# Attention over four images: image 0's first attention in two halves of the queries, and the score maxima of images 2 and 3 computed earlier

## The chip, the cores and the metric

One core of one Trainium2 chip runs the whole program. The metric is device time in microseconds (us) of one execution.

## The reference, cut to what matters

Four images of 64 channels and 1024 pixels each go through three steps.

```python
xf = x.reshape(b, c, n)                         # b=4, c=64, n=1024
q, k, v = (einsum('mc,bcn->bmn', w, xf) for w in (wq, wk, wv))   # m=32
att = softmax(einsum('bmi,bmj->bij', k, q), axis=2)              # 1024 x 1024 an image
x = x + einsum('cm,bmn->bcn', wo, einsum('bij,bmj->bmi', att, v))
t = tokens(x)                                   # 4 x 1024 x 64
z = layernorm(t)
t = t + softmax(z z^T) z                        # second attention
z = layernorm(t)                                # router, top 2 of 8 experts
t = t + gated sum of the two chosen experts of z
```

The first softmax has large scores and so needs the maximum of each row; the second one uses a constant shift.

## The kernel before, in words

**Tiles.** An image has 8 tiles of 128 tokens. Attention 1 of an image has two passes. The maxima pass: TensorE makes the scores of a tile with tokens on the partitions (`max_scores`, L465), VectorE reduces each tile to its row maxima (`row_max`, L1070), negates them and splits them in a high and a low part (`negate_max`, L1076 and L1078), TensorE turns them into a row (`max_row`, L474), and ScalarE and VectorE copy one half each of this row into `kst` (L874, L1083). The score pass: the transposed scores with the maximum already subtracted (`scores1`, L483), the exponential on ScalarE (`exp1`, L877) and the weighted sum of the values on TensorE (`weigh_pair1`, two tiles a call, L490). A score tile needs the whole row, so that no `scores1` of an image begins before the last of its maxima. After it come the output projection (`project_out`, L527), the tokens and their layer norm on VectorE (`tokens1`, `stats_of_1`, `normalize1`, with one power on GpSimd), their transposition (`u_transposed`, L538), attention 2 (`scores2` L551 and L552, `exp2` L880, `weigh_pair2` L490), its transposition (`copy_att2` L889 on ScalarE, `att2_transposed` L566 on TensorE), the second norm, the router (`w_transposed`, `route`), the choice of two experts (`top2` on VectorE with `gap_exp`, L905, on ScalarE), and the experts (`experts` L596, `weigh_experts` L1209 on VectorE, sums on GpSimd).

**Before the maxima** of an image its q and k are projected (`project_qk`), rounded by ScalarE (`round_q` L857, `round_k` L860) and split by VectorE (`split_q` L1062, `split_k` L1067); `project_v` (L454, L455) makes the values, which ScalarE copies (`values`, L865 and L869). `round_x` (L854) and GpSimd prepare x.

**The ring.** TensorE writes nearly all results into three buffers of PSUM of two banks each. `ORDER` (L44 to L72) lists every use of the ring in the order of TensorE's program; use n takes buffer n mod 3, and `take` makes TensorE wait until use n - 3 has been read (`release` names the semaphore). So a tile in the list is bound to the one that stands three places ahead of it, whoever reads that one.

**Order.** There is no loop or planner: each engine has its instructions written out in one order, and executes them in it. The order interleaves images. The stages are those of the list: HEAD (load, image 0's maxima), FIRST (image 0's scores 1, image 1's maxima), SECOND (image 1's scores 1), THIRD (image 0's scores 2, image 2's maxima), FOURTH (image 2's scores 1), FIFTH (image 1's scores 2, image 3's maxima, image 0's experts), SIXTH (image 3's scores 1), SEVENTH and EIGHTH (scores 2 of images 2 and 3), TAIL. `keep_clock(n)` (L632) issues n matmuls on a constant tile whose result nobody reads.

Of the kernel before, what the change touches and what calls it, by code (L numbers as in the profile page):

```python
# [24 lines left out]
P = 128  # L25
# [10 lines left out]
DEEP = 4  # L36


def per_tile(name, b):
# [4 lines left out]
HEAD = [("w3", 0), ("q", 0), ("k", 0), ("vx", 0)] + per_tile("mx", 0) + [("q", 1), ("k", 1), ("mr", 0)]  # L44

FIRST = [("st0", 0), ("st1", 0), ("mx0", 1), ("st2", 0), ("mx1", 1), ("st3", 0), ("mx2", 1), ("mx3", 1), ("st4", 0),
         ("mx4", 1), ("st5", 0), ("mx5", 1), ("st6", 0), ("mx6", 1), ("st7", 0), ("mx7", 1), ("vx", 1), ("mr", 1),
         ("po", 0)]
# [4 lines left out]
THIRD = [("s0", 0), ("s1", 0), ("po", 1), ("mx0", 2), ("s2", 0), ("mx1", 2), ("s3", 0), ("mx2", 2), ("s4", 0),  # L53
         ("mx3", 2), ("s5", 0), ("q", 3), ("uT", 1), ("mx4", 2), ("s6", 0), ("k", 3), ("mx5", 2), ("s7", 0),
         ("mx6", 2), ("mx7", 2), ("vx", 3), ("mr", 2)]

FOURTH = [(f"st{j}", 2) for j in range(6)] + [("wT", 0), ("st6", 2), ("st7", 2), ("rt", 0)]

FIFTH = [("s0", 1), ("s1", 1), ("po", 2), ("mx0", 3), ("s2", 1), ("mx1", 3), ("s3", 1), ("mx2", 3), ("e0", 0),
         ("s4", 1), ("mx3", 3), ("s5", 1), ("uT", 2), ("e1", 0), ("mx4", 3), ("s6", 1), ("mx5", 3), ("e2", 0),  # L60
         ("s7", 1), ("mx6", 3), ("mx7", 3), ("e3", 0), ("mr", 3)]
# [8 lines left out]
          ("rt", 2), ("s7", 3)]  # L70
TAIL = [("e0", 2), ("e1", 2), ("e2", 2), ("wT", 3), ("e3", 2), ("rt", 3), ("e0", 3), ("e1", 3), ("e2", 3), ("e3", 3)]
# [12 lines left out]
def build(nc, x, wq, wk, wv, wo, rw, rb, ew, eb, out):  # L84
    ctx = ExitStack()
    with ctx:
# [56 lines left out]
        prob1 = sb("prob1", [P, DEEP, N])  # L143
        prob2 = sb("prob2", [P, DEEP, N])
# [65 lines left out]
        s_mrow = sem("maxrow_ready")  # L210
        s_p1 = sem("probs1_ready")
# [49 lines left out]
        def release(name, b):  # L261
# [4 lines left out]
            if name in table:  # L266
                return table[name]
            family, at = {"mx": s_mx, "st": s_p1, "s": s_p2, "e": s_prod}[name[:-1]], int(name[-1])
# [155 lines left out]
        def _(pe):  # L424
# [44 lines left out]
            def max_row(b):  # L469
                buf = take("mr", b)  # L470
                pe.wait_ge(s_nm, 2 * (b + 1))
# [15 lines left out]
            def weigh(acc, stationary, prob, j, s_p, s_sum, b):  # L487
                pe.wait_ge(s_p, T * b + j + 1)
                for h in range(2):
                    mm = pe.matmul(acc[h * C:(h + 1) * C, :], stationary[:, j, :], prob[:, j % DEEP, h * CHUNK:(h + 1) * CHUNK],  # L490
                                   start=(j == 0), stop=(j == T - 1))
# [3 lines left out]
            def weigh1(b, j):  # L495
# [4 lines left out]
                weigh(acc1, val[b % 2], prob1, j, s_p1, s_av1, b)  # L500

            def weigh2(b, j):
# [6 lines left out]
                weigh(sum2[b], u[b % 2], prob2, j, s_p2, s_av2, b)  # L509
# [135 lines left out]
            for tile in range(T):  # L645
# [12 lines left out]
            scores1(0, 1)  # L658
            max_scores(1, 0)
            scores1(0, 2)  # L660
# [718 lines left out]
```

## Time and profile before

| | |
|---|---|
| median of 3 runs | 226.32 us (226.16 to 229.27) |
| the profiled execution, its own time | 226.99 us |
| its span | 225.3 us |
| TensorE busy | 206.7 us, 92% |
| VectorE, ScalarE, GpSimd busy | 143.6, 107.4, 62.5 us |
| mean granted TensorE clock | 0.992 |

The profiled execution's time is its span and 1.7 us around it; it is 0.67 us above the median. Busy shares of TensorE are upper bounds of work, since the ends of pipelined matmuls are modelled and overlap: the distance from one start to the next is what a matmul costs in a row of them.

### The profile page before, as it was taken

The numbers are of one execution on the slowest core, as the hardware profiler recorded it, in microseconds if no ns is written. First come the engines' busy times: TensorE is split into PE (matmuls) and PEld (weight loads), VectorE is DVE, ScalarE is ACT, GpSimd is POOL, SyncE is SP. The second block draws the span as 40 slices with busy tenths as digits, with TensorE's granted clock in tenths as the row PEclk, the third lists the DMA queues.
The fourth block names the chain that finished last, engine by engine and source line by source line (L and its number), as shares of the span: only waits on it lengthen the run. The fifth ranks groups of instructions, "written<-read, shape, count | busy, mean of one in ns | idle before, by whom it ended". The sixth has DMA issues, their size and how long they took to land.

```text
span 225.3 us, 2932 instructions
## 1 busy us (share of the span) xinstructions
PE 206.7 (92%) x1075; PEld 105.0 (47%) x1075; DVE 143.6 (64%) x358; ACT 107.4 (48%) x166; POOL 62.5 (28%) x75
## 2 busy tenths in 40 slices
PE   7899899998999887989997999899999999898993
PEld 2554443653643333544443534434445433376873
DVE  2589864587509854472589468936784272698970
ACT  2631664397684473176543623685645566301110
POOL 8140000053211200003002445830177751017260
PEclk9999999999999999699999999999999999999999
DMA  4752000000000000000000000010000002000021
GB/s 104 143 144 44 3 0 0 0 1 3 1 0 0 0 3 0 0 0 0 3 0 1 0 3 0 1 47 0 3 0 0 0 3 48 0 0 3 0 47 47
DMA packets 3341, 3.67 MB, mean 16 GB/s; under 512 B 2176, under 2 KB 2432, under 8 KB 3328
## 3 DMA queue, kind: packets, MB, share of 16 engines
q1 hardware_dynamic: 3328, 3.50, 7.0%
q8 instruction: 8, 0.13, 0.3%
q14 instruction: 5, 0.04, 0.1%
HBM read 2.45 MB, written 1.05 MB: 16 GB/s over the span
## 4 chain that ended last, share of the span: by engine, by line
PE 69%; DVE 18%; ACT 7%; issue 2%; DMA 2%; POOL 1%; SPq 0%; DVEq 0%; POOLq 0%
PE acc L490 25%; DVE rowmax L1070 7%; PE ring L596 7%; PE ring L551 6%; PE ring L483 6%; PE ring L552 5%; PE ring L465 4%; PE acc L626 3%; DMA xin<-in_x 2%; PE ring L454 2%; PE ring L455 2%; ACT prob L880 2%; DVE qst L1062 2%; DVE stats L1103 1%; ACT prob L877 1%
## 5 line engine op out<-in xcount | busy, mean ns | idle before, releaser
L880 ACT ACTIVATE prob<-ring,shift 128x1024 f32<-128x1024 f32 x32 | 35.6, 1112 | 35.0 <-PE ring L552 34.9
L1070 DVE TENSOR_REDUCE rowmax<-ring 128x1 f32<-128x1024 f32 x32 | 37.6, 1218 | 11.6 <-PE ring L465 11.6
L877 ACT ACTIVATE prob<-ring 128x1024 f32<-128x1024 f32 x32 | 32.0, 1025 | 16.3 <-PE ring L483 16.3
L368 POOL TENSOR_TENSOR sm<-sm,minus_half 128x8 f32<-128x8 f32 x8 | 15.8, 1974 | 84.5 <-DVE sm L1113 84.5
L490 PE MATMUL acc<-prob,u 128*64 128x512 f32 x128 | 32.5, 627 | 1.0 <-ACT prob L880 1.0
L490 PE MATMUL acc<-prob,val 128*64 128x512 f32 x128 | 31.1, 605 | 1.0 <-ACT prob L877 1.0
L551 PE MATMUL ring<-zst 128*128 128x512 f16 x64 | 24.6, 384 | 3.8 <-DVE rowmax L1070 2.7
L465 PE MATMUL ring<-qst,kst 96*128 96x512 f32 x64 | 22.4, 439 | 2.0 <-DVE kst L1067 1.0
L552 PE MATMUL ring<-zsw,zst 128*128 128x512 f16 x64 | 24.3, 379 | 0.0
L1209 DVE TENSOR_TENSOR prod<-ring,gate 128x1024 f32<-128x1024 f32 x16 | 19.4, 1220 | 7.3 <-PE ring L596 6.8
L483 PE MATMUL ring<-kst,qst 98*128 98x512 f32 x64 | 20.8, 423 | 3.0 <-DVE kst L1083 1.2
L374 POOL TENSOR_TENSOR xst<-xin,xst 64x1024 fp32r<-64x1024 f32 x3 | 7.5, 2515 | 45.7 <-ACT xst L854 45.7
L465 PEld LDWEIGHTS ring<-qst,kst 96*128 96x128 f32 x64 | 10.3, 188 | 14.0 <-DVE rowmax L1070 4.8
L483 PEld LDWEIGHTS ring<-kst,qst 98*128 98x128 f32 x64 | 10.5, 188 | 12.4 <-ACT prob L877 4.9
L490 PEld LDWEIGHTS acc<-prob,u 128*64 128x64 f32 x128 | 7.9, 141 | 17.2 <-issue 14.9
L490 PEld LDWEIGHTS acc<-prob,val 128*64 128x64 f32 x128 | 7.6, 135 | 16.6 <-issue 11.4
L551 PEld LDWEIGHTS ring<-zst 128*128 128x128 f16 x64 | 6.2, 97 | 19.2 <-issue 7.1
L380 POOL TENSOR_TENSOR half<-prod 128x512 f32<-128x512 f32 x8 | 10.5, 1314 | 16.2 <-DVE prod L1209 16.1
L596 PE MATMUL ring<-e,w_hi 64*128 64x512 f32 x64 | 13.4, 447 | 0.2 <-ACT prob L880 0.2
L596 PE MATMUL ring<-e,w_lo 64*128 64x512 f32 x64 | 11.9, 396 | 0.0
L632 PE MATMUL acc<-filler 128*128 128x512 f16 x29 | 10.4, 478 | 1.5 <-DVE filler L1213 1.5
L419 POOL TENSOR_TENSOR prod<-prod 128x512 f32<-128x512 f32 x6 | 7.5, 1278 | 5.9 <-DVE prod L1209 5.0
(155 smaller groups left out, 311.3 us busy)
## 6 DMA issues: line engine op xcount, KB each, us to landing
xin<-in_x SPq DMA_DIRECT2D x8, 256.0 KB, 4.0
out<-ob SPq DMA_DIRECT2D x6, 128.0 KB, 2.3
e_in<-in_L_ffn_expert_w SPq DMA_DIRECT2D x2, 128.0 KB
out<-ob SPq DMA_DIRECT2D x4, 64.0 KB, 2.0
eb_in<-in_L_ffn_expert_b SPq DMA_DIRECT2D x8, 2.0 KB
wo<-in_L_conv_wo SPq DMA_DIRECT2D x2, 8.0 KB, 2.4
r_in<-in_L_ffn_router_w SPq DMA_DIRECT2D x2, 2.0 KB
w<-in_L_conv_wq SPq DMA_DIRECT2D x1, 16.0 KB, 3.5
```

The lines of the kernel that those rows point to most:

```text
L368: pool.tensor_tensor(sm[:, 3, :], sm[:, 2, :], minus_half[:, :], ALU.pow).then_inc(s_rs, 1)
L380: pool.tensor_tensor(half[:, :, :, :], p[:, 0:E // 2], p[:, E // 2:E], ALU.add).then_inc(s_half, 1)
L465: mm = pe.matmul(buf[:, h, :], kst[home][0:ROW, col(tile):col(tile) + P], qst[home][0:ROW, h * CHUNK:(h + 1) * CHUNK], start=True, stop=True)
L483: mm = pe.matmul(buf[:, h, :], qst[home][0:ROW + 2, col(j):col(j) + P], kst[home][0:ROW + 2, h * CHUNK:(h + 1) * CHUNK], start=True, stop= ...
L490: mm = pe.matmul(acc[h * C:(h + 1) * C, :], stationary[:, j, :], prob[:, j % DEEP, h * CHUNK:(h + 1) * CHUNK], start=(j == 0), stop=(j == ...
L551: pe.matmul(buf[:, h, :], z, straight[:, h * CHUNK:(h + 1) * CHUNK], start=True, stop=False)
L552: mm = pe.matmul(buf[:, h, :], z, swapped[:, h * CHUNK:(h + 1) * CHUNK], start=False, stop=True)
L596: mm = pe.matmul(buf[:, h, :], w[rows, g * P:(g + 1) * P], e[rows, :], start=(n == 0), stop=(n == 3))
L877: act.activation(prob1[:, j % DEEP, :], flat(filled(act, f"st{j}", b)), ACT.Exp).then_inc(s_p1, 1)
L880: act.activation(prob2[:, j % DEEP, :], flat(filled(act, f"s{j}", b)), ACT.Exp, bias=shift[:, :], accum_out=rsum2[b % 2][:, j:j + 1]).then ...
L1070: dve.tensor_reduce(rowmax[:, tile:tile + 1], flat(filled(dve, f"mx{tile}", b)), AX.X, ALU.max).then_inc(s_mx, 1)
L1209: dve.tensor_tensor(prod[:, g].rearrange("p e h c -> p h e c"), buf.rearrange("p h (e c) -> p h e c", c=C), gates, ALU.mult).then_inc(s_pr ...
```

## The change

**Image 0's attention 1 in halves.** Its maxima are taken in the order 0, 2, 4, 6, 1, 3, 5, 7 (`BY_HALF`). `col` places the even tiles in columns 0 to 511 and the odd ones in 512 to 1023, so the first four maxima complete the first half of the row. `negate_half` and `max_row_half` do the row in two halves; the first is copied by ScalarE, the second by VectorE. `scores1_half` fills one buffer with the scores of two key tiles against one half of the queries, and `exp1_half` takes the exponential of it: ha0 to ha3 for the first half, hb0 to hb3 for the second. The sizes of the instructions stay, 128x1024 for each exponential. `prob1` has 8 places for 4, so that all first halves can lie there until the second come. k of image 1 is projected behind the second row half, not ahead of the row. There are 25 filler matmuls where there were 29.

**Images 2 and 3.** `max_scores` of image 2 begins in SECOND (3 tiles), and ends in THIRD (5); that of image 3 begins at the end of THIRD (2), goes on in FOURTH (3) and ends in FIFTH (3). The reductions on VectorE move with them, ahead of `tokens1` and between the steps of the norms. `max_row` of both images is issued ahead of the last work of the stage before, where it was at the end of it. `att2_transposed` of images 0 and 1 moves from ahead of `scores1(b, 0)` to behind it, and `copy_att2` on ScalarE from ahead of the row's copy to behind the first exponential. q, k and v of image 3, and `experts` and `weigh_experts` of image 0, shift by a few places.

**The end.** `experts(2, 0)` is issued ahead of the last `weigh_pair2(3, 6)`, not behind it.

```diff
-DEEP = 4
+DEEP1 = 8
+DEEP2 = 4
+BY_HALF = [0, 2, 4, 6, 1, 3, 5, 7]
...
-HEAD = [("w3", 0), ("q", 0), ("k", 0), ("vx", 0)] + per_tile("mx", 0) + [("q", 1), ("k", 1), ("mr", 0)]
-FIRST = [("st0", 0), ("st1", 0), ("mx0", 1), ("st2", 0), ("mx1", 1), ("st3", 0), ("mx2", 1), ("mx3", 1), ("st4", 0),
-         ("mx4", 1), ("st5", 0), ("mx5", 1), ("st6", 0), ("mx6", 1), ("st7", 0), ("mx7", 1), ("vx", 1), ("mr", 1),
...
+FIRST = [("hb0", 0), ("k", 1), ("hb1", 0), ("hb2", 0), ("mx0", 1), ("mx1", 1), ("hb3", 0), ("mx2", 1), ("mx3", 1),
+         ("mx4", 1), ("mx5", 1), ("mx6", 1), ("vx", 1), ("mx7", 1), ("mr", 1), ("po", 0)]
 SECOND = [("st0", 1), ("st1", 1), ("st2", 1), ("q", 2), ("st3", 1), ("k", 2), ("st4", 1), ("vx", 2), ("st5", 1),
-          ("uT", 0), ("st6", 1), ("st7", 1)]
...
-FOURTH = [(f"st{j}", 2) for j in range(6)] + [("wT", 0), ("st6", 2), ("st7", 2), ("rt", 0)]
-FIFTH = [("s0", 1), ("s1", 1), ("po", 2), ("mx0", 3), ("s2", 1), ("mx1", 3), ("s3", 1), ("mx2", 3), ("e0", 0),
...
+THIRD = [("s0", 0), ("mx3", 2), ("s1", 0), ("po", 1), ("mx4", 2), ("s2", 0), ("q", 3), ("s3", 0), ("mx5", 2),
+         ("k", 3), ("s4", 0), ("mx6", 2), ("s5", 0), ("uT", 1), ("mx7", 2), ("s6", 0), ("vx", 3), ("s7", 0),
+         ("mr", 2), ("mx0", 3), ("mx1", 3)]
+FOURTH = [("st0", 2), ("st1", 2), ("mx2", 3), ("st2", 2), ("st3", 2), ("mx3", 3), ("st4", 2), ("st5", 2), ("wT", 0),
+          ("st6", 2), ("st7", 2), ("rt", 0), ("mx4", 3)]
+FIFTH = [("s0", 1), ("s1", 1), ("po", 2), ("mx5", 3), ("s2", 1), ("s3", 1), ("mx6", 3), ("s4", 1), ("e0", 0),
...
-          ("rt", 2), ("s7", 3)]
-TAIL = [("e0", 2), ("e1", 2), ("e2", 2), ("wT", 3), ("e3", 2), ("rt", 3), ("e0", 3), ("e1", 3), ("e2", 3), ("e3", 3)]
+          ("rt", 2), ("s7", 3), ("e0", 2)]
+TAIL = [("e1", 2), ("e2", 2), ("wT", 3), ("e3", 2), ("rt", 3), ("e0", 3), ("e1", 3), ("e2", 3), ("e3", 3)]
 ORDER = HEAD + FIRST + SECOND + THIRD + FOURTH + FIFTH + SIXTH + SEVENTH + EIGHTH + TAIL
...
+                return s_mrow, int(name[-1]) + 1
+            if name[:2] == "ha":
+                return s_ha, int(name[-1]) + 1
+            if name[:2] == "hb":
+                return s_p1, 2 * int(name[-1]) + 2
+            if name[:2] == "mx" and b == 0:
+                return s_mx, BY_HALF.index(int(name[-1])) + 1
...
+            def max_row_half(half):
+                buf = take(f"mr{half}", 0)
+                pe.wait_ge(s_nm, 2 * (half + 1))
+                for tile in range(half, T, 2):
+                    c = col(tile)
+                    mm = pe.matmul(flat(buf)[0:ROW + 2, c:c + P], nmax[:, tile, :], ident_r[:, :], start=True, stop=True)
+                mm.then_inc(s_fill, 1)
...
+            def scores1_half(half, g):
+                buf = take(("ha", "hb")[half] + str(g), 0)
+                if g == 0:
+                    pe.wait_ge(s_mrow, half + 1)
+                for n in range(2):
+                    j = 2 * g + n
+                    mm = pe.matmul(buf[:, n, :], qst[0][0:ROW + 2, col(j):col(j) + P],
+                                   kst[0][0:ROW + 2, chunk(half)], start=True, stop=True)
                 mm.then_inc(s_fill, 1)
...
+            for n, tile in enumerate(BY_HALF[0:4]):
                 max_scores(0, tile)
-                if tile >= RING - 1:
+                if n >= RING - 1:
                     keep_clock(2)
+            max_scores(0, 1)
             pe.wait_ge(s_wol, 2 * 16)
             pe.transpose(acc2[:, 0:C], wo4[:, :, :].rearrange("p a m -> p (a m)"), ident[0:C, 0:C]).then_inc(s_woT, 1)
+            keep_clock(2)
+            max_row_half(0)
+            scores1_half(0, 0)
+            for g in range(1, 4):
+                max_scores(0, 2 * g + 1)
+                scores1_half(0, g)
+                keep_clock(2)
             project_qk("q", 1)
+            max_row_half(1)
+            keep_clock(2)
+            scores1_half(1, 0)
             project_qk("k", 1)
-            keep_clock(3)
-            max_row(0)
-            keep_clock(3)
-            scores1(0, 0)
-            scores1(0, 1)
+            scores1_half(1, 1)
+            weigh_pair1(0, 0)
+            scores1_half(1, 2)
             max_scores(1, 0)
-            scores1(0, 2)
-            weigh_pair1(0, 0)
             max_scores(1, 1)
-            scores1(0, 3)
+            weigh_pair1(0, 2)
+            scores1_half(1, 3)
             max_scores(1, 2)
             max_scores(1, 3)
-            scores1(0, 4)
-            weigh_pair1(0, 2)
+            weigh_pair1(0, 4)
             max_scores(1, 4)
-            scores1(0, 5)
             max_scores(1, 5)
-            scores1(0, 6)
-            weigh_pair1(0, 4)
             max_scores(1, 6)
-            scores1(0, 7)
+            project_v(1)
             max_scores(1, 7)
             weigh_pair1(0, 6)
-            project_v(1)
             max_row(1)
             project_out(0)
...
             scores1(1, 5)
             u_transposed(0)
+            max_scores(2, 0)
             scores1(1, 6)
             weigh_pair1(1, 4)
+            max_scores(2, 1)
             scores1(1, 7)
+            max_scores(2, 2)
             scores2(0, 0)
...
+            scores1(2, 0)
+            att2_transposed(0)
+            scores1(2, 1)
+            max_scores(3, 2)
+            scores1(2, 2)
+            weigh_pair1(2, 0)
+            scores1(2, 3)
+            max_scores(3, 3)
+            scores1(2, 4)
+            weigh_pair1(2, 2)
+            scores1(2, 5)
+            w_transposed(0)
+            scores1(2, 6)
+            weigh_pair1(2, 4)
+            scores1(2, 7)
+            route(0)
+            max_scores(3, 4)
...
             scores2(3, 7)
+            experts(2, 0)
             weigh_pair2(3, 6)
-            experts(2, 0)
             att2_transposed(3)
             gates_transposed(2)
...
+            act.activation(kst[0][ROW:ROW + 2, 0:CHUNK], buf[ROW:ROW + 2, 0, :], ACT.Copy).then_inc(s_mrow, 1)
+            def exp1_half(half, g):
+                buf = filled(act, ("ha", "hb")[half] + str(g), 0)
+                probs = act.activation(prob1[:, 2 * g:2 * g + 2, chunk(half)], buf[:, :, :], ACT.Exp)
+                if half:
+                    probs.then_inc(s_p1, 2)
+                else:
+                    probs.then_inc(s_ha, 1)
+            for g in range(4):
+                exp1_half(0, g)
             round_q(1)
+            exp1_half(1, 0)
             round_k(1)
-            max_row(0)
-            for j in range(4):
-                exp1(0, j)
...
             exp2(0, 0)
             copy_agg(1)
-            for j in range(1, 5):
-                exp2(0, j)
+            exp2(0, 1)
+            exp2(0, 2)
+            round_q(3)
+            exp2(0, 3)
+            round_k(3)
+            exp2(0, 4)
             copy_high(1)
             exp2(0, 5)
-            round_q(3)
             stack_swapped(1)
             exp2(0, 6)
-            round_k(3)
+            values(3)
             exp2(0, 7)
-            values(3)
-            for b in (2, 3):
...
-                copy_att2(b - 2)
-                max_row(b)
-                for j in range(T):
-                    exp1(b, j)
-                    if b == 3 and j == 3:
-                        result(0)
-                    if j == 5:
-                        round_w(b - 2)
-                gap_exp(b - 2)
+            max_row(2)
+            exp1(2, 0)
+            copy_att2(0)
+            for j in range(1, 6):
+                exp1(2, j)
+            round_w(0)
+            exp1(2, 6)
+            exp1(2, 7)
+            gap_exp(0)
...
+            max_row(3)
+            exp1(3, 0)
+            copy_att2(1)
+            for j in range(1, 4):
...
+                for tile in BY_HALF[4 * half:4 * half + 4]:
+                    row_max(0, tile)
+                negate_half(half)
+            buf = filled(dve, "mr1", 0)
+            dve.tensor_copy(kst[0][ROW:ROW + 2, CHUNK:N], buf[ROW:ROW + 2, 1, :]).then_inc(s_mrow, 1)
             split_q(1)
-            max_row(0)
...
                               tile_mask[:, :].unsqueeze(2).to_broadcast([T * E, T, C]), ALU.mult).then_inc(s_es, 1)
             stack_u(0)
-            tokens1(1)
             row_max(2, 0)
-            stats_of_1(1)
             row_max(2, 1)
             row_max(2, 2)
+            row_max(2, 3)
+            tokens1(1)
+            row_max(2, 4)
+            stats_of_1(1)
+            split_q(3)
             normalize1(1)
-            row_max(2, 3)
-            split_q(3)
+            row_max(2, 5)
+            split_k(3)
+            row_max(2, 6)
             stack_u(1)
-            row_max(2, 4)
-            split_k(3)
-            row_max(2, 5)
-            row_max(2, 6)
             row_max(2, 7)
             negate_max(2)
             max_row(2)
+            row_max(3, 0)
+            row_max(3, 1)
             tokens2(0)
+            row_max(3, 2)
             stats_of_2(0)
+            row_max(3, 3)
             normalize2(0)
             split_w(0)
+            row_max(3, 4)
             top2(0)
             tokens1(2)
+            row_max(3, 5)
             stats_of_1(2)
-            row_max(3, 0)
-            row_max(3, 1)
+            row_max(3, 6)
             normalize1(2)
-            row_max(3, 2)
             weigh_experts(0, 0)
-            row_max(3, 3)
             stack_u(2)
-            weigh_experts(0, 1)
-            row_max(3, 4)
-            row_max(3, 5)
-            weigh_experts(0, 2)
-            row_max(3, 6)
             row_max(3, 7)
             negate_max(3)
+            weigh_experts(0, 1)
+            weigh_experts(0, 2)
+            max_row(3)
             weigh_experts(0, 3)
-            max_row(3)
```

## Rows read from the trace of the kernel before

**Rows 1.** Windows of FIRST to FIFTH, PE: stretch, length, busy (count), clock, DMA share, GB/s.
```profile
26.28:46.48 20.20, 19.42 (x94) 1.00 0.00 1
46.48:62.38 15.90, 14.53 (x79) 1.00 0.01 2
62.38:97.48 35.10, 30.86 (x152) 0.95 0.00 0
97.48:108.30 10.82, 10.53 (x46) 1.00 0.00 0
108.30:141.50 33.20, 31.19 (x168) 1.00 0.01 1
```

**Rows 2.** Timeline, THIRD: start, length, engine, line, operation, tiles, [idle before, releaser].
```profile
67.82 0.21 DVE L1090 RECIPROCAL rinv<-ring 128x8 f32<-128x8 f32 x1 [7.10 <-PE ring L527]
...
68.13 0.39 PE L551 MATMUL ring<-zst 128*128 128x512 f16 x1
68.35 0.38 PE L552 MATMUL ring<-zsw,zst 128*128 128x512 f16 x1
...
74.28 0.39 PE L551 MATMUL ring<-zst 128*128 128x512 f16 x1 [1.25 <-DVE rowmax L1070]
...
82.19 0.39 PE L551 MATMUL ring<-zst 128*128 128x512 f16 x1 [1.10 <-DVE qst L1062]
...
88.56 0.73 PE L465 MATMUL ring<-qst,kst 96*128 96x512 f32 x2 [1.02 <-DVE kst L1067]
```

**Rows 3.** Timeline, end of THIRD: the last weighing and the row of image 2's maxima.
```profile
92.55 3.22 PE L490 MATMUL acc<-prob,u 128*64 128x512 f32 x8
95.69 0.91 PE L474 MATMUL ring<-ident_r,nmax 128*98 128x128 f32 x8
```

**Rows 4.** Chain of waits: start, length, what; steps of TensorE in an unbroken row.
```profile
27.01 0.47 PE ring L465 x2
...
27.95 1.87 PE acc L490 x8
```

**Rows 5.** Timeline, HEAD: image 0's maxima, then image 1's q and image 0's scores.
```profile
13.37 9.14 DVE L1070 TENSOR_REDUCE rowmax<-ring 128x1 f32<-128x1024 f32 x8 [0.88 <-PE ring L465]
...
23.03 1.22 DVE L1062 TENSOR_TENSOR qst<-ring,qst 32x1024 fp32r<-32x1024 f32 x1
...
24.28 0.70 DVE L1083 CAST kst<-ring 2x512 fp32r<-2x512 f32 x1
...
25.12 0.70 PE L483 MATMUL ring<-kst,qst 98*128 98x512 f32 x2 [0.43 <-DVE kst L1083]
...
26.28 0.73 PE L483 MATMUL ring<-kst,qst 98*128 98x512 f32 x2 [0.46 <-DVE kst L1067]
```

**Rows 6.** Timeline, ScalarE at the end of FIRST.
```profile
42.95 0.60 ACT L885 ACTIVATE agg<-acc 128x512 f32<-128x512 f32 x1 [1.32 <-PE acc L490]
```

**Rows 7.** Timeline, ScalarE in SECOND: the exponential of image 1's tile 5.
```profile
60.29 1.03 ACT L877 ACTIVATE prob<-ring 128x1024 f32<-128x1024 f32 x1
```

**Rows 8.** Timeline, FIFTH: ScalarE behind image 0's gap, and TensorE's longest wait.
```profile
110.73 0.21 ACT L905 ACTIVATE gm<-gm 128x8 f32<-128x8 f32 x1 [1.24 <-DVE gm L1177]
110.85 1.10 ACT L880 ACTIVATE prob<-ring,shift 128x1024 f32<-128x1024 f32 x1
...
119.41 0.39 PE L551 MATMUL ring<-zst 128*128 128x512 f16 x1 [1.47 <-DVE rowmax L1070]
```

**Rows 9.** Timeline, ScalarE around the start of SIXTH.
```profile
139.86 0.60 ACT L889 ACTIVATE att<-acc 128x512 f32<-128x512 f32 x1 [3.16 <-PE acc L490]
...
142.27 2.85 ACT L877 ACTIVATE prob<-ring 128x1024 f32<-128x1024 f32 x3 [0.99 <-PE ring L483]
```

**Rows 10.** Timeline, start of TAIL: the last weighing, then VectorE on expert group 0.
```profile
195.14 1.08 PE L490 MATMUL acc<-prob,u 128*64 128x512 f32 x4 [0.96 <-ACT prob L880]
...
197.39 1.23 DVE L1209 TENSOR_TENSOR prod<-ring,gate 128x1024 f32<-128x1024 f32 x1 [0.79 <-PE ring L596]
...
198.53 0.68 DVE L1144 TENSOR_TENSOR odiv<-acc,rinv 128x512 f32<-128x512 f32 x1
```

More of the change, by code:

```diff
@@ L705, in _ @@
             scores2(0, 3)
[L706 removed]
+            max_scores(2, 5)
+            project_qk("k", 3)
             scores2(0, 4)
             weigh_pair2(0, 2)
[L709 removed]
+            max_scores(2, 6)
             scores2(0, 5)
[L711 removed]
             u_transposed(1)
[L713 removed]
+            max_scores(2, 7)
             scores2(0, 6)
             weigh_pair2(0, 4)
[L716 to L717 removed]
+            project_v(3)
@@ new lines, in _ @@
+            weigh_pair1(2, 6)
+            scores2(1, 1)
+            project_out(2)
+            max_scores(3, 5)
+            scores2(1, 2)
+            gates_transposed(0)
+            weigh_pair2(1, 0)
+            scores2(1, 3)
+            max_scores(3, 6)
+            expert_bias(0)
+            scores2(1, 4)
+            weigh_pair2(1, 2)
+            experts(0, 0)
+            scores2(1, 5)
+            u_transposed(2)
+            max_scores(3, 7)
+            experts(0, 1)
+            scores2(1, 6)
@@ new lines, in _ @@
+            weigh_pair2(1, 4)
+            experts(0, 2)
+            scores2(1, 7)
+            max_row(3)
+            experts(0, 3)
+            weigh_pair2(1, 6)
+            scores1(3, 0)
+            att2_transposed(1)
+            scores1(3, 1)
+            scores1(3, 2)
+            weigh_pair1(3, 0)
+            scores1(3, 3)
+            y_transposed(0)
+            scores1(3, 4)
+            weigh_pair1(3, 2)
+            scores1(3, 5)
+            w_transposed(1)
+            scores1(3, 6)
@@ L773, in _ @@
+            weigh_pair1(3, 4)
+            scores1(3, 7)
+            route(1)
             scores2(2, 0)
@@ L953, in _ @@
                 act.activation(r_blk[rows, h, 0, :], r_in[rows, :], ACT.Copy).then_inc(s_er, 1)
-            for j in range(4, T):
-                exp1(0, j)
             copy_agg(0)
@@ L976, in _ @@
             copy_agg(1)
[L977 to L978 removed]
+            exp2(0, 1)
[4 more added lines that the diff above has]
+            exp2(0, 4)
             copy_high(1)
             exp2(0, 5)
[L981 removed]
             stack_swapped(1)
             exp2(0, 6)
[L984 removed]
+            values(3)
             exp2(0, 7)
[L986 to L1011 removed]
+            max_row(2)
+            exp1(2, 0)
[6 more added lines that the diff above has]
+            gap_exp(0)
+            exp2(1, 0)
+            copy_agg(2)
+            exp2(1, 1)
+            exp2(1, 2)
+            copy_gates(0)
+            exp2(1, 3)
+            copy_bias(0)
+            exp2(1, 4)
+            copy_high(2)
+            exp2(1, 5)
+            stack_swapped(2)
+            exp2(1, 6)
+            exp2(1, 7)
+            max_row(3)
+            exp1(3, 0)
+            copy_att2(1)
+            for j in range(1, 4):
+                exp1(3, j)
+            result(0)
+            exp1(3, 4)
+            exp1(3, 5)
+            round_w(1)
+            exp1(3, 6)
+            exp1(3, 7)
+            gap_exp(1)
             exp2(2, 0)
@@ L1238, in _ @@
                     dve.tensor_tensor(lo, ring[rows, k, h, :], lo.bitcast(F32), ALU.subtract).then_inc(s_split, 1)
-            for tile in range(T):
-                row_max(0, tile)
             dve.wait_ge(s_const, 4)
-            negate_max(0)
+            for half in range(2):
+                for tile in BY_HALF[4 * half:4 * half + 4]:
[3 more added lines that the diff above has]
+            dve.tensor_copy(kst[0][ROW:ROW + 2, CHUNK:N], buf[ROW:ROW + 2, 1, :]).then_inc(s_mrow, 1)
             split_q(1)
-            max_row(0)
             split_k(1)
```

128 lines of the change are left out of this document (37 added, 91 removed).

## The prediction

> **What bounds the kernel now.** I read the windows by stage first, then the chain of waits, then the timeline around each wait of TensorE that ended on another engine. The windows show TensorE busy for nearly all of every stage, and the longest stages are THIRD with 35.10 us and FIFTH with 33.20 us [rows 1]. Busy overstates work, so I count work by the steps of unbroken rows: a tile of maxima or of scores 1 takes 0.47 us, a weighed pair 1.87 us [rows 4], a tile of scores 2 four steps of 0.22, 0.87 us [rows 2]. THIRD then holds 8 x 0.87 + 5 x 1.87 + 8 x 0.47 = 20.1 us, 0.47 for the score tile its window begins with, 1.9 for q and k (four tiles' worth of matmuls), 1.8 for v, and some 3.4 for the small ones (projection, u, row of maxima, att: 0.7 to 0.9 each): 27.6 us, so about 7.5 us of it are waits or a slow clock. The same count gives FIFTH 29.3 us (with 4.5 of experts) and 3.9 of waits, and FOURTH 9.9 and 0.9.
>
> The reader is to see what the waits of THIRD are: TensorE stands 1.25 us for a row maximum, 1.10 for the split of q, 1.02 for that of k, while VectorE had stood idle for 7.10 us just before 67.82 [rows 2]. Then comes the end of the stage: the last maxima are reduced one behind the other, TensorE has little to do, and the next weighing takes 3.22 us at the lower clock against the 1.87 of any other [rows 3, 4]. THIRD's mean clock is 0.95, that of the other stages 1.00 [rows 1]. So the bound is TensorE, plus what VectorE's list makes it wait for where maxima, token work and splits meet.
>
> **The change, part by part.** I followed the new lists with the durations of the rows, an instruction at a time, on the three engines.
>
> HEAD and FIRST. Before, VectorE reduces from 13.37 to 22.51, the row is copied by 24.98, scores 1 begin at 25.12 and, after 0.43 and 0.46 us of waits, run from 26.28 [rows 5]. After, the fourth reduction ends at 17.9 (8 take 9.14, so one 1.14), the two negations and the half row follow, and the first half's scores start near 19.8. But the remaining maxima now share the ring with the half tiles: VectorE stands about 1.4 us for tile 3, and the last maximum is reduced at 25.15 instead of 22.51. The second row half is copied by 27.15 (0.70), hb0 starts at 27.3, the split of image 1's q (1.22) can only follow and ends at 28.35, and its k is projected behind that. Image 1's maxima start at 32.3, where they start near 27 before [rows 4]. TensorE has then done four half tiles more (1.9) and k less (0.9). From there it is bound by its own work, with waits of about 2 us, and ScalarE's copy of the aggregate, at 42.95 before [rows 6], comes at 44.65, since the last weighing now stands behind project_v; values and row follow it. SECOND starts at 47.2 for 46.48: **+0.7 us**. The low end of this term is -1.7 (both waits of 0.4 and what else TensorE stands in FIRST, 20.20 less 19.42 [rows 1]), the high end +2.2 (hb0 at 27.3 against 25.12, nothing made up). The four fillers less are taken at nothing: TensorE waits there anyway; without that cover they would give 4 x 0.22.
>
> SECOND and THIRD. The first three maxima of image 2 fall in VectorE's idle stretch and cost TensorE 3 x 0.47 here and as much less in THIRD. Tile 6 of scores 1 now stands three places behind tile 5, whose exponential starts at 60.29 and takes 1.03 [rows 7]: a wait of 1.0. The first tile of scores 2 waits for maximum 1: 0.55. In THIRD q of image 3 goes early, and its k waits for split_q behind tokens1, one maximum and the norm's statistics: 1.35; small waits add 0.5. Sum 3.4, for 7.5 before, since the last maximum is reduced while TensorE still has v, a score tile and two maxima of image 3, and the slow clock goes with that hole. Two maxima come in (0.94), att's transposition leaves (0.7). 3.4 - 7.5 + 0.2 = **-3.8**. Ends: no new wait, -7.2; each of three more tiles with one of 1.1 as in [rows 2], -0.5.
>
> FOURTH. Three maxima (1.4) and the transposition of att (0.5) come in. The transposition stands behind the first scores, and ScalarE copies att only behind the first exponential: TensorE stands for latency, 1.03 and 0.60, together 1.9 us, of which 0.3 replaces a wait of before, and some others shrink. +1.4 + 0.5 + 1.3 = **+3.2**; ends +1.9 (work alone) and +3.8. VectorE has three more reductions ahead of top2(0).
>
> FIFTH. Five maxima (2.35) and att (0.7) are gone. The waits go from 3.9, of which 1.47 is one for a row maximum [rows 8], to about 1.9. The largest is new: top2(0) comes 1.0 later, gap_exp waits for it, and exp2(1, 0), the copy of the aggregate and project_out(2) are queued behind it on ScalarE; even before, this exponential started only 0.12 after gap_exp [rows 8]. That costs 1.3. -2.35 - 0.7 - 2.0 = **-5.0**; ends -6.9 (no wait left) and -3.1 (waits as before).
>
> SIXTH. The same step: before, the copy of att (0.60) ran ahead of the scores and three exponentials 0.95 apart followed [rows 9]; now TensorE stands 1.9 for it, 0.5 of which the earlier first exponential gives back; att adds 0.5. **+1.9**; ends 0 and +2.4.
>
> TAIL. TensorE stands 0.96 us for the last exponential, then weighs, then makes expert group 0 (1.13), and VectorE's product (1.23) of it delays the tokens to 198.53 [rows 10]. With the group in that wait the product starts when top2 ends at 196.5 and the tokens when att is turned, near 197.75: **-0.8**; ends -1.1 and 0. SEVENTH and EIGHTH are unchanged and shift. The other moves (projections of image 3, weigh_experts) are covered by TensorE's own work. DMAs and SP are untouched, and GpSimd's expert sums of image 0 get earlier.
>
> Sum: 0.7 - 3.8 + 3.2 - 5.0 + 1.9 - 0.8 = **-3.8 us**. The profiled execution took 226.99, so 223.2 by it; it stands 0.67 above the median of 226.32, so 222.5 as a median.
>
> **A rule against the change.** No weighing but one ran at the lower clock, although waits of 1.0 to 1.5 us precede several steps [rows 2, 8]; I take the new waits of 1.9 as harmless, and the sum has no slow step. The Trainium skill, "TensorE: Matmul & The Clock Gate", section "A second HAM failure mode: psum-queue depth-cycling", tells of short idles between groups of matmuls, from cycling through PSUM, that let the clock fall again and again; this change puts more such idles in. By it the sum would end higher, as in the clock's rival below.
>
> **The rivals.**
> *Fewer waits.* My walk adds each latency in full, and its 3.4, 1.9 and twice 1.9 us of waits rest on steps a few tenths apart. If a third of these 9 go, the kernel is 3 us quicker still: 219.5. For it: TensorE has fallen back on its own work after almost every wait. Against: the two for att are hard, since nothing stands between them.
> *The halves cost twice.* k of image 1 late and nothing made up: +2.2 for +0.7, 224.0.
> *The clock.* If it falls behind each of the two waits for att, each costs what it cost in THIRD, 3.22 - 1.87 = 1.35 [rows 3, 4]: 225.2. Against: before, waits of 1.47 did nothing.
> *The ring.* Eleven maxima of images 2 and 3 stand in new places, each behind the readers of other engines and with a tile bound to it three places on. Without any new wait the change would give 3.8 + 3.4 = 7.2 us; if each of them makes TensorE wait over 7.2 / 11 = 0.65 us it is slower than before, and at the 1.10 of [rows 2] it gives 226.3 - 7.2 + 12.1 = 231.2. Against: of the eight in THIRD before, few made TensorE wait [rows 2].
> *It does not do what it says.* The row of maxima still ends each stage and the holes only move: 226.
>
> **How the numbers follow.** Forecast 222.5 with 0.45, fewer waits 0.27, halves 0.10, clock 0.08, ring 0.05, nothing 0.05. 2% of 226.32 is 4.5 us, about what a measurement of this kernel tells from no change, so faster means below 221.8 and slower above 230.8. Below 221.8 lie nearly all of the fewer waits and a third of the forecast's own spread: 0.40. Above 230.8 about half of the ring: 0.03. The rest, 0.57, is within. The range of 8 in 10 reaches from 219.3, near the fewer waits' time, to 225.7, past the clock's.
>
> **What would show it.** Right: first half scores near 19.8 and SECOND at 47; no PE clock below 1.00 around 90; scores 1 of image 2 near 94.3 and of image 3 near 136.4 (141.5 before); att's transposition in both places with an idle of 1.9 ended by ScalarE; k of image 3 waiting for split_q. Wrong: image 2's scores after 96, waits on row maxima of over 0.6 us at many tiles, or SECOND before 46, where the halves would have paid.

## The result

The changed kernel takes 228.51 us (median of 20 runs, 226.54 to 231.47); the kernel before beside it 226.36 (20 runs). The ratio is 1.0088, interval [1.0065, 1.011]: 2.0 us slower, where 3.8 us less had been forecast. The ratios here and below leave out executions over 1.5% above the fastest of the same kernel. The profiled execution took 229.89 us with a span of 228.2, for 226.99 and 225.3 before.

To hold the two against each other I cut both spans at the same five events: TensorE's first maximum, the first scores 1 of images 1, 2 and 3, the first scores 2 of image 2. Windows of the kernel before; columns are stretch, length, TensorE's busy time (count), granted clock, DMA share, GB/s:

```profile
0.00:12.63 12.63, 10.00 (x37) 1.00 0.54 111
12.63:46.48 33.85, 32.18 (x147) 1.00 0.13 32
46.48:97.48 51.00, 45.39 (x228) 0.97 0.00 1
97.48:141.53 44.05, 41.71 (x212) 1.00 0.00 1
141.53:153.63 12.10, 11.80 (x57) 1.00 0.09 22
153.63:225.30 71.67, 65.64 (x399) 1.00 0.05 12
```

The same six of the changed kernel:

```profile
0.00:13.07 13.07, 9.54 (x36) 0.87 0.54 107
13.07:49.42 36.35, 32.35 (x146) 0.95 0.12 29
49.42:97.58 48.16, 44.33 (x231) 1.00 0.00 1
97.58:141.81 44.23, 41.78 (x209) 0.96 0.00 1
141.81:157.36 15.55, 13.95 (x62) 0.89 0.07 17
157.36:228.20 70.84, 65.55 (x399) 1.00 0.05 12
```

Only two stretches got shorter, the third (51.00 to 48.16) and the tail. The clock column shows a part of why the second, fourth and fifth did not: it was 1.00 in them before and is 0.95, 0.96 and 0.89 now. The hole at the end of THIRD with its slow weighing [rows 3] is gone, as forecast; three new slow places have come. (The first stretch, 0.87 here, varies: in the runs below the maxima start between 11.7 and 15.1 us in kernels with the same instructions up to there.) Two-microsecond windows of the changed kernel at these places, the same columns:

```profile
22.00:24.00 2.00, 2.00 (x6) 0.50 0.00 0
...
100.00:102.00 2.00, 2.00 (x8) 0.54 0.00 0
...
144.00:146.00 2.00, 1.85 (x7) 0.64 0.00 0
146.00:148.00 2.00, 2.00 (x6) 0.51 0.00 0
```

Each of these falls of the clock to about half stands just behind a wait that the change put in. Timeline of the changed kernel (start, length, engine, line, operation, tiles, [idle before, releaser]), at the first half row and at att's transposition for images 0 and 1:

```profile
19.05 0.53 PE L495 MATMUL ring<-ident_r,nmax 128*98 128x128 f32 x4 [1.29 <-DVE nmax L1169]
...
20.35 0.70 PE L505 MATMUL ring<-kst,qst 98*128 98x512 f32 x2 [0.77 <-ACT kst L999]
20.89 0.62 PE L477 MATMUL ring<-qst,kst 96*128 96x512 f32 x2
...
22.43 1.41 PE L477 MATMUL ring<-qst,kst 96*128 96x512 f32 x2
...
99.92 0.91 PE L598 MATMUL acc<-ident,att 128*128 128x128 f32 x4 [1.60 <-ACT att L945]
...
144.15 0.78 PE L598 MATMUL acc<-ident,att 128*128 128x128 f32 x4 [1.60 <-ACT att L945]
...
146.57 2.61 PE L522 MATMUL acc<-prob,val 128*64 128x512 f32 x8
```

A pair of maximum matmuls takes 1.41 us at 22.43, for 0.62 at 20.89; a weighed pair 2.61, for 1.94 at 139.95.

The 20 executions of the changed kernel say the same without a profile: the three with a mean clock of 0.989 to 0.99 took 226.54 to 226.78 us; eleven with 0.982 to 0.985 from 227.49 to 228.69; one with 0.977 228.78; four with 0.967 to 0.97 from 229.58 to 229.89, and a fifth, at 0.969, 231.47. The kernel before, in the 70 executions beside the experiments below, ran 53 times at 0.990 to 0.992, nine times at 0.969 to 0.977 (229.0 to 229.4 us), and twice at 0.998, in 224.51 and 224.65 us. So even where the changed kernel falls least it takes as long as the median of the kernel before, 226.36.

### The profile page after: what moved, and what is told of

It is laid out like the page before. It is cut to its first block, busy times and chain, and to the rows that moved or that the text cites. A ratio compares the mean times of both kernels' runs of the same rounds, so it can differ in the third digit from the quotient of the medians.

```text
span 228.2 us, 2932 instructions
## 1 busy us (share of the span) xinstructions
PE 207.5 (91%) x1071; PEld 107.3 (47%) x1071; DVE 145.1 (64%) x360; ACT 107.3 (47%) x166; POOL 61.2 (27%) x75
## 4 chain that ended last, share of the span: by engine, by line
PE 74%; DVE 13%; ACT 7%; DMA 2%; issue 2%; POOL 1%; SPq 0%; DVEq 0%; POOLq 0%
PE acc L522 24%; PE ring L583 6%; PE ring L628 6%; PE ring L477 5%; PE ring L515 5%; PE ring L584 5%; DVE rowmax L1151 4%; PE acc L658 3%; PE ring L455 2%; PE ring L505 2%; DMA xin<-in_x 2%; PE ring L559 2%; PE ring L466 2%; DVE qst L1143 2%; PE ring L467 2%
## 5 line engine op out<-in xcount | busy, mean ns | idle before, releaser
L1151 DVE TENSOR_REDUCE rowmax<-ring 128x1 f32<-128x1024 f32 x32 | 38.3, 1220 | 15.6 <-PE ring L477 15.4
L522 PE MATMUL acc<-prob,val 128*64 128x512 f32 x128 | 31.8, 618 | 0.0
L522 PE MATMUL acc<-prob,u 128*64 128x512 f32 x128 | 31.0, 606 | 0.0
L515 PE MATMUL ring<-kst,qst 98*128 98x512 f32 x48 | 18.2, 472 | 2.3 <-DVE qst L1143 1.3
L477 PEld LDWEIGHTS ring<-qst,kst 96*128 96x128 f32 x64 | 11.4, 199 | 6.9 <-issue 2.7
L515 PEld LDWEIGHTS ring<-kst,qst 98*128 98x128 f32 x48 | 8.7, 212 | 10.9 <-ACT prob L933 5.3
L628 PE MATMUL ring<-e,w_hi 64*128 64x512 f32 x64 | 12.6, 442 | 0.0
L1003 ACT ACTIVATE prob<-ring 128x1024 f32<-128x1024 f32 x8 | 8.2, 1023 | 7.8 <-PE ring L505 7.7
L628 PE MATMUL ring<-e,w_lo 64*128 64x512 f32 x64 | 11.2, 394 | 0.0
L664 PE MATMUL acc<-filler 128*128 128x512 f16 x25 | 9.2, 489 | 1.5 <-DVE filler L1304 1.5
```

The source lines that it names most:

```text
L477: mm = pe.matmul(buf[:, h, :], kst[home][0:ROW, col(tile):col(tile) + P], qst[home][0:ROW, h * CHUNK:(h + 1) * CHUNK], start=True, stop=True)
L515: mm = pe.matmul(buf[:, h, :], qst[home][0:ROW + 2, col(j):col(j) + P], kst[home][0:ROW + 2, h * CHUNK:(h + 1) * CHUNK], start=True, stop= ...
L628: mm = pe.matmul(buf[:, h, :], w[rows, g * P:(g + 1) * P], e[rows, :], start=(n == 0), stop=(n == 3))
L1151: dve.tensor_reduce(rowmax[:, tile:tile + 1], flat(filled(dve, f"mx{tile}", b)), AX.X, ALU.max).then_inc(s_mx, 1)
```

## The experiments

Ratios are those to the kernel before beside them. "Second part" is all of the change from SECOND on, "halves" the change to HEAD and FIRST.

**1 and 2. The two parts alone.** Lists and engine orders of one kernel up to FIRST, of the other from SECOND on.

> Only the first part of the change (HEAD and FIRST in halves of the queries; from SECOND on the order of before). Theory CLOCK (the loss is new idle of TensorE behind which its clock falls: once in HEAD, once behind each wait for att): this kernel holds HEAD's fall and its later start of SECOND, so it is slower than before by 2 to 4 us, 228.5 to 230.5, with a stretch at the lower clock near 21 to 25 us. Rival RING (the loss is in waits of TensorE for row maxima of images 2 and 3 in their new places): the halves cost the forecast's +0.7, 227.0, and no lower clock need show.

> Only the second part (HEAD and FIRST of before; maxima of images 2 and 3 early; the expert group in TAIL too). CLOCK: two falls behind the waits for att remain, some 1.2 us each; the rest of the forecast holds (-4.5 + 2.4): faster by about 2, 224.3, with the scores 1 of image 2 near 94 and of image 3 near 137. RING: as slow as the whole change or slower than before, 227 or more, with waits on row maxima over 0.6 us at several tiles.

Halves: 1.0071 [1.0032, 1.0111], 228.0 us and so between the 227.0 of RING and the 228.5 of CLOCK, the stretch 20 to 26 us at a clock down to 0.50. This ratio rests on four executions, of 227.24 to 228.99 us; the other eight took 231.68 to 232.66. Second part: 0.9968 [0.9934, 1.0003]. So the halves alone lose and the second part alone does not; that the two make up the whole is not shown (1.0039 together, for 1.0088). The second part gives a third of what was expected of it alone, with scores 1 of image 2 at 93.81 and of image 3 at 136.87 as expected, and then 15.55 us, not 12.1, to the scores 2 of image 2. Its profiled execution has a fall behind the second of the waits for att and none behind the first. RING is wrong: the largest wait for a row maximum in any kernel with the second part is 0.4 us.

**3. Fillers in the waits for att**, in the whole change.

```diff
             scores1(2, 0)
+            pe.wait_ge(s_agg, 2)
+            keep_clock(4)
             att2_transposed(0)
```

> The changed kernel, with four fillers (0.87 us) in each of the two waits for att, whose length stays. CLOCK: no fall behind them, about 1.2 us each given back, 226.2 for the changed kernel's 228.5. RING, or a fall that costs nothing: as the changed kernel, 228.5.

1.0052 [1.0013, 1.009] for 1.0088: 0.8 us of the 2.3 expected, with overlapping intervals. In the trace no window behind either wait is below full clock, and the stretches are 43.07 and 14.83 us for 44.23 and 15.55. The falls cost 1.2 and 0.7 us there. That the fillers kept them away is not shown by one trace, since experiment 7 has none there without fillers; but none of this kernel's 12 executions has a mean clock under 0.985, and 6 of the changed kernel's 20 are at 0.977 or under. This execution also has a fall that no other has, from 44 to 50 us at the end of FIRST, where TensorE had stood for no more than 0.39 us at once in the ten microseconds before, and had just issued the 16 short matmuls of `project_v`.

**4 and 5. att's transposition moved**, in the second part alone: behind the next two tiles (4), or back ahead of the scores, its copy too (5).

```diff
+            att2_transposed(0)
             scores1(2, 0)
-            att2_transposed(0)
...
+            copy_att2(0)
             exp1(2, 0)
-            copy_att2(0)
```

> The second part alone, with the transposition of att behind the next scores and maximum (or scores), so that TensorE works while ScalarE makes the exponential and copies att. CLOCK with the waits: both waits of 1.6 to 1.9 us shrink to under 0.8 and no fall follows, so 3 us or more better than the second part alone: 221.5 to 222.5. RING: no gain over the second part alone, since the wait moves to the next reader of the ring.

> The second part alone, with att's transposition and its copy back ahead of the first scores and the first exponential of images 2 and 3, as before the change. NORM (att's late transposition delays the tokens, the norm and then w_transposed, for which TensorE stands 1.58 us in SIXTH of the kernel with att later): that wait goes, SIXTH takes 12.1 to 13 us from its first scores to the first scores 2 (15.5 in the second part alone, 14.8 with att later), the clock stays up, and the time is 221.5 to 223. Rival CLOCK ALONE: nothing over the kernel with att later, which had no fall: 225.

Later: 0.9918 [0.9886, 0.9951], 1.1 us under the second part alone, where 3 or more had been expected. First: 0.9822 [0.9792, 0.9851], 222.3 us, as expected. No fall in either behind att. With it later TensorE stood elsewhere; timeline of that kernel, SIXTH:

```profile
139.33 0.66 PE L566 MATMUL acc<-ident,att 128*128 128x128 f32 x4 [0.67 <-ACT att L909]
...
140.67 1.27 POOL L393 TENSOR_TENSOR y<-yres,ybias 128x512 f32<-128x512 f32 x1
140.82 1.67 DVE L1183 TENSOR_TENSOR tok<-odiv,tok 128x512 f32<-128x512 f32 x1
...
146.70 0.69 DVE L1188 TENSOR_TENSOR wn<-cen,sm 128x512 f32<-128x512 f32 x1 [1.61 <-POOL sm L368]
147.54 0.63 PE L574 MATMUL ring<-ident,wn 128*128 128x128 f32 x4 [1.58 <-DVE wn L1188]
```

The second norm begins with att's transposition; what delays it comes back as 1.58 us in front of w_transposed. SIXTH, from its first scores 1 to the first scores 2, was 12.2 us long with att first, and 14.8 with att later; some of this is the transposition itself, which with att first stands ahead of that stretch.

**6 and 14. Fillers in HEAD**, in the halves alone; one kernel twice, since the profiled execution of the first had a span of 392.5 us and can't be read against the others.

```diff
-            keep_clock(2)
+            keep_clock(6)
             max_row_half(0)
+            keep_clock(2)
             scores1_half(0, 0)
```

> The first part alone, with four fillers more ahead of the first half row and two behind it, in the waits of 1.29 and 0.77 us. CLOCK: no stretch below full clock at 21 to 25 us, image 1's scores 1 start 1.4 us earlier than without (near 48.2), and the time falls by 1.4. If the half-row's waits matter and not the clock: as without the fillers, ratio 1.007.

> The halves alone with fillers in HEAD, once more. CLOCK in HEAD: no stretch at the lower clock at 20 to 25 us and a ratio under the 1.0071 of the halves without them. If the 1.0142 was no accident: over 1.01 again, with a slow stretch elsewhere that the trace shows.

1.0142 [1.0108, 1.0176] and 1.0117 [1.0068, 1.0165], for 1.0071 without; each interval overlaps with that of the halves. Windows of HEAD and FIRST, then of SECOND and THIRD, of the halves alone (experiment 1) and with the fillers (14):

```profile
13.19:49.53 36.34, 32.34 (x145) 0.95 0.13 29
49.53:102.30 52.77, 47.07 (x232) 0.94 0.00 1
```

```profile
12.66:47.63 34.97, 32.32 (x150) 1.00 0.13 31
47.63:100.37 52.74, 47.02 (x232) 0.94 0.00 1
```

The fall in HEAD is gone, and with it 1.4 us. Both kernels still have the hole of THIRD, and in both executions the clock is low there for longer than in the kernel before: 52.77 and 52.74 us for 51.00. The fillers changed nothing at that hole. The ratios can't tell more: that of the halves leaves out eight of 12 executions, all over 231.6 us, and of the 11 with fillers beside the one of 392.5 only one took that long (232.59), so that the median of all executions is 231.71 without the fillers and 230.05 and 229.11 with them. In the times it stays open whether the fillers pay in this kernel.

**7 and 8. GpSimd behind VectorE**, in the whole change, and the second of its two waits in the second part with att first.

```diff
+            pool.wait_ge(s_tk1, 1)
             split_x(2)
...
+                else:
+                    pool.wait_ge(s_tk2, 2)
                 pool.tensor_tensor(y[:, :, :], yres[:, :, :], ybias[:, :, :], ALU.add).then_inc(s_y, 1)
```

> The changed kernel, with GpSimd made to wait in two places until VectorE has written the tokens (split of image 2's x behind tok of image 0; y of image 0 behind tok of image 1). LOCK (VectorE's addition of two SBUF operands stands until GpSimd's instruction, begun just before, is over: 2.54 and 1.53 us for 0.69): both take 0.69, and the time falls by 0.5 to 2, the larger if the split of q behind it was what TensorE waited for. Otherwise: the same 228.5, and the durations show chance.

> The second part alone with att first, and y of image 0 on GpSimd behind tok of image 1. LOCK: tok of image 1 takes 0.69 where it would take 1.67, but with att first it may start before y anyway: 0 to 1 us under the kernel with att first.

1.0083 [1.0043, 1.0122] and 0.9846 [0.9818, 0.9874], for 1.0088 and 0.9822 without: nothing gained in the times, where 0.5 to 2 us and 0 to 1 had been expected. Timeline of the changed kernel:

```profile
50.29 2.37 POOL L386 TENSOR_TENSOR xst<-xin,xst 64x1024 fp32r<-64x1024 f32 x1 [32.63 <-ACT xst L910]
...
50.67 2.54 DVE L1187 TENSOR_TENSOR tok<-tdiv,xt 128x512 f32<-128x512 f32 x1
```

and of the one with the waits:

```profile
49.48 0.69 DVE L1190 TENSOR_TENSOR tok<-tdiv,xt 128x512 f32<-128x512 f32 x1
...
51.35 1.34 DVE L1200 TENSOR_TENSOR sm<-stats 128x8 f32<-128x8 f32 x1
```

The addition that stood until GpSimd was done (52.66 and 0.55 more) runs in 0.69; 1.2 us are lost again one step later (`sm` took 0.17), TensorE stands 0.70 us for the split of x that GpSimd was made to begin later, and the stretch to image 2's scores is 48.56 us for 48.16. Only image 1's, in SIXTH, pays: 13.99 us for the 14.83 of experiment 3, both without a fall.

This profiled execution of experiment 7 happened to have no fall behind its first 14 us, and so shows the change, with these two waits of GpSimd in it, at full clock:

```profile
13.27:48.23 34.96, 30.97 (x145) 1.00 0.13 30
48.23:96.79 48.56, 44.41 (x232) 1.00 0.00 1
96.79:139.86 43.07, 40.44 (x210) 1.00 0.00 1
139.86:153.85 13.99, 12.39 (x63) 1.00 0.08 19
153.85:224.60 70.75, 65.51 (x399) 0.99 0.05 12
```

**9. att late, in the kernel before:** that one step, nothing else of the change.

```diff
-                att2_transposed(b - 2)
                 scores1(b, 0)
+                att2_transposed(b - 2)
```

> The kernel before, with one step of the change alone: att's transposition behind the first scores of images 2 and 3, and its copy behind their first exponential. NORM and the waits: TensorE stands 1.6 us at each, and the norm behind it comes late for w_transposed: slower by 2 to 4 us, 228.5 to 230.5. Rival (att's place costs only with the early maxima): within 1 us of the kernel before.

1.02 [1.0135, 1.0264], from three of six executions: 4.5 us for two places, where 2 to 4 had been expected. In its profiled execution, which took 234.48 us, the two waits are 1.60 us each, and the clock is low from 90 to 97 and, behind the first wait, from 100 to 107; a weighed pair at 103.23 takes 3.68 us. Behind the second wait it is 1.00, and SIXTH takes 13.95 us for 12.10: so much att late costs there without a fall.

**10. gap_exp behind the first exponential of FIFTH**, in the second part with att first.

```diff
-            gap_exp(0)
-
             exp2(1, 0)
+            gap_exp(0)
```

> The second part alone with att first, and on ScalarE gap_exp(0) behind exp2(1, 0). QUEUE: the exponential no longer stands for top2 (it began at 112.57, its scores were there at 110.7), the aggregate's copy and project_out(2) come some 0.8 us earlier, and TensorE's wait of 0.85 us for it goes: 0.5 to 0.9 us under the second part with att first (ratio 0.982). Rival: top2 waits for its exponential instead, and nothing is gained.

0.9781 [0.9734, 0.9828], median 221.39, for 0.9822: as expected in size, but with overlapping intervals. In the trace the wait for the aggregate is gone. Before the edit (kernel of experiment 8) and with it:

```profile
112.57 1.10 ACT L902 ACTIVATE prob<-ring,shift 128x1024 f32<-128x1024 f32 x1
...
114.39 1.13 PE L529 MATMUL ring<-wo_blk,agg 128*128 128x130 f32 x8 [0.85 <-ACT agg L907]
```

```profile
111.47 1.11 ACT L900 ACTIVATE prob<-ring,shift 128x1024 f32<-128x1024 f32 x1 [1.23 <-PE ring L552]
...
114.10 1.11 PE L527 MATMUL ring<-wo_blk,agg 128*128 128x130 f32 x8
```

**11, 12 and 13. The whole change mended:** att first (11), with HEAD's fillers (12), with gap_exp later too (13).

> The whole change, with att's transposition and copy back ahead of the first scores and exponential of images 2 and 3. NORM: gains what it gave the second part alone (1.4% from 0.9968 to 0.9822), so 225.0 to 225.5, ratio 0.994. Rival RING: 228 still.

> As the kernel with the whole change and att first, with four fillers more ahead of the first half row of image 0's maxima and two behind it. CLOCK in HEAD: no stretch at the lower clock at 20 to 25 us, and 1 us faster than without, 224.3. Rival: the fillers only delay the half row, as in the halves alone with fillers (ratio 1.0142 for 1.0071): slower.

> The whole change with att first, the fillers in HEAD and gap_exp(0) behind exp2(1, 0). If the halves cost 0.7 us at full clock: 0.3% above the second part with att first and the gap later (0.9781), so ratio 0.981, 222.1. If they cost more: 0.985 or over.

0.9939 [0.991, 0.9968], 0.9851 [0.9811, 0.9891], 0.9832 [0.9797, 0.9867]. Windows of 11, then of 12:

```profile
20.00:22.00 2.00, 2.00 (x7) 0.50 0.00 0
22.00:24.00 2.00, 2.00 (x8) 0.70 0.00 0
```

```profile
20.00:22.00 2.00, 1.97 (x9) 1.00 0.00 0
22.00:24.00 2.00, 2.00 (x10) 1.00 0.00 0
```

Here the fillers are worth 0.9%, 1.8 us by the medians where 1 had been expected, and the clock bears them out in every execution: 0.983 to 0.992 in the 12 without, 0.999 to 1.0 in the 12 with them. The stretch of HEAD and FIRST takes 36.35, 36.34 and 36.36 us in the traces with a fall in it (the changed kernel, 1, 11), and 34.96 to 34.98 in those without (7, 12, 13, 14). The halves then cost 0.3% (12 against 5) to 0.5% (13 against 10), 0.7 to 1.1 us, with overlapping intervals. The fastest kernel of all by the median is 10, without the halves, 2.2% under the kernel before.

## Why the prediction was wrong

**The step that failed** is "I take the new waits of 1.9 as harmless, and the sum has no slow step". The premise was a row with an idle of 1.47 and no fall behind it [rows 8]. But the four profiled executions that keep the waits for att at 1.60 us (the changed kernel, 2, 7, 9) have a fall behind four of the eight; and in HEAD, where the waits are shorter still (1.29 and 0.77), four of the five without more fillers have one (the changed kernel, 1, 3 and 11, not 7). The fall that the kernel before has itself, in THIRD, told as much: it stands behind waits of 1.02 [rows 2] and 0.52 us. Timeline and windows of the kernel before:

```profile
89.82 0.73 PE L465 MATMUL ring<-qst,kst 96*128 96x512 f32 x2 [0.52 <-DVE rowmax L1070]
```

```profile
92.00:94.00 2.00, 2.00 (x7) 0.50 0.00 0
94.00:96.00 2.00, 2.00 (x9) 0.71 0.00 0
```

That is the rival of the clock, and it had 0.08 of chance and two places; the third, HEAD, I had not counted. The prices, from stretches with and without a fall: 36.35 - 34.96 = 1.4 us in HEAD and FIRST, 1.2 in FOURTH and FIFTH, 0.7 in SIXTH, 3.3 together. The rule that the prediction weighed is that short idles between groups of matmuls, from cycling through PSUM, let the clock fall (the Trainium skill, "TensorE: Matmul & The Clock Gate", "A second HAM failure mode: psum-queue depth-cycling"). The traces agree that idles of 0.8 to 1.6 us can go ahead of a fall, against my reading of the rows; that cycling through the ring is what does it no run shows, since the waits at the three new places are for ScalarE's and VectorE's results.

**The falls are half of the miss.** The profiled execution has all three and took 2.9 us more of span than that of the kernel before, 6.7 more than forecast. Of these, 3.3 are the falls; 1.0 is SECOND and THIRD, 0.8 FOURTH and FIFTH, 0.8 an addition on VectorE in SIXTH, 0.4 HEAD and FIRST, and 0.4 was there at the first maximum. Without a fall the change would still have missed: the span of experiment 7's profiled execution is 0.7 us under that of the kernel before, not 3.8, and its time, 226.36, is the median of the kernel before.

**HEAD and FIRST, +0.7.** At full clock 34.96 for 33.85: +1.1 (and 0.7 to 1.1 by experiments 12 and 13). The sign was right, the size 0.4 short; the first half scores began at 20.35, with 19.8 forecast and 0.44 of the difference already there at the first maximum.

**SECOND and THIRD, -3.8.** Measured -2.8 (51.00 to 48.16). Three waits are those of the walk: 0.86 at tile 6 of scores 1 (1.0 forecast), 0.38 at the first scores 2 (0.55), 1.01 in the projections of image 3 (1.35). A fourth, 1.33 at image 1's scores for the split of q, was 0.97 before and is 0.97 again in experiment 7. The term that was too large is the 7.5. It was what a count of work left over of THIRD, and not read from waits: the window has 35.10 - 30.86 = 4.24 us of idle [rows 1], and the slow weighing adds 1.35. Over the whole stretch TensorE's idle went from 5.61 to 3.83, 1.8 less; with the 1.35 and the 0.2 of added work that is -2.9, for the -2.8 measured. (Idle is what busy time leaves, and busy is an upper bound, so the true waits may be somewhat longer; no run was made for this term.)

**FOURTH and FIFTH, +3.2 - 5.0 = -1.8.** At full clock 43.07 for 44.05, -1.0; measured +0.2 with the fall. The same term failed: the 3.9 of waits in FIFTH was left over of a count too, where the window has 33.20 - 31.19 = 2.01 us of idle [rows 1]. In both stages together TensorE's busy time went down by 1.3 at full clock (1.15 forecast), but its idle went up from 2.34 to 2.63, where 0.7 less had been forecast. The queue behind gap_exp was there: the last matmul of the scores begins at 114.80, the exponential at 117.04. The wait for the aggregate behind it is 0.85, for a cost of 1.3 in the forecast.

**SIXTH, +1.9.** Measured +3.5: 15.55 for 12.10. Without the fall it is 14.83 (experiment 3), +2.7, and 13.99 only when GpSimd waits for VectorE (experiment 7), which is the +1.9 of the forecast. The 0.84 between is VectorE's addition behind GpSimd, 1.53 us for 0.69, of which the prediction had said that GpSimd's sums "get earlier" and nothing of what they then meet.

**TAIL, -0.8.** 71.67 to 70.84, with the product at 200.30 and the tokens behind it at once: right.

**The price of att.** The prediction booked 1.9 us of wait twice, and did not ask whether the step was worth them. It was the worst of the change: alone 2.0% (experiment 9), and in the whole change its return gives 1.5% (11). The forecast should also have seen what delaying it does to the norm, though in the changed kernel itself w_transposed waited 0.3 us at most; it was 0.66 in experiment 3, and 1.58 when att was put later still.

**What stays open.** The profiled execution of experiment 7 took 224.6 us of span, but that kernel's median is no better than the changed one's: its 12 executions have mean clocks from 0.968 to 0.991. Executions of one kernel differ in how many falls they have; why one has them and the next not was not tried. Nor was it tried whether it is the wait alone: the fall of THIRD and that of experiment 3 in FIRST both come with the short matmuls of `project_v`. In the times, experiment 3 shows only 0.8 us for two falls, within the intervals of no effect.

## What to carry to other kernels

Price a new wait of TensorE twice, once as idle and once as a slow stretch behind it, and ask for every moved step that ScalarE must serve whether TensorE has other work to do meanwhile. Fillers in a wait can keep the clock up: in HEAD they gave 0.9% in a kernel that had no other hole. In a kernel that kept one, the traces give the same 1.4 us, but its executions differ by more than that, and the times did not show the gain.

Waits that are to be saved must be read as idle from the trace. What a count of work leaves over of a stage is not all waits: here it promised 7.5 us in THIRD where idle and slow clock were 5.6, and 3.9 in FIFTH where idle was 2.0.

When a change is several at once, run its steps alone: here one of them, a transposition and a copy one step later, cost 2.0% alone, and the change without it was 0.6% faster than the kernel before.

## What the runs showed of the hardware

- The clock fell to half behind waits of 1.60 us in four cases of eight, and behind waits of 1.29 and 0.77 us in four of five, in kernels with the same waits there; within one kernel mean clock and time go together, 0.99 with 226.6 and 0.97 with 229.7 us. One fall cost 0.7 to 1.4 us.
- Fillers in the two waits of HEAD, with att first: 12 executions at a mean clock of 0.999 to 1.0 (experiments 12 and 13), for 0.983 to 0.992 in the 12 without (11).
- A VectorE addition of two SBUF operands that starts 0.4 us after a GpSimd instruction on SBUF takes 2.54 us for 0.69, ending 0.55 after it. In the kernel before VectorE was first and GpSimd took 2.82 us for 2.37. The Trainium skill, "SBUF — State Buffer", section "Who interferes with whom", says that a VectorE instruction with two SBUF inputs contends with a GpSimd instruction that reads SBUF, and that the port pair they share is an exclusive lock for whoever starts first. The trace agrees, 52.66 + 0.55 = 53.21.
- It holds for small instructions too: a VectorE step on 128x8 with both inputs in SBUF, 0.17 us otherwise, took 1.34 behind GpSimd in experiment 7.
